# Convolution kernel: normalisation two steps ahead, high parts in front of signs, one more pair of products split by columns

## The reference: two layers on eight images

```python
def _L0_conv_ref(x, depthwise_weights, pointwise_weights, attention_weights, global_attention_weight):
    dw = lax.conv_general_dilated(x, depthwise_weights, ..., feature_group_count=C)   # 3x3, padding 1
    A = jax.nn.softmax(attention_weights, axis=1)
    att = jnp.einsum('cd,bdhw->bchw', A, dw)
    pw = jnp.einsum('kc,bchw->bkhw', pointwise_weights[:, :, 0, 0], att)
    G = jax.nn.softmax(global_attention_weight, axis=1)
    return jnp.einsum('cd,bdhw->bchw', G, pw)

def _L1_conv_ref(x, w):
    xb = jnp.sign(x)
    wc = jnp.clip(w, -1.0, 1.0)
    mean_val = jnp.mean(jnp.abs(wc), axis=(1, 2, 3), keepdims=True)
    bw = jnp.sign(wc) * mean_val
    return lax.conv_general_dilated(xb, bw, ...)                                      # 3x3, padding 1

x = x + _L0_conv_ref(_gn(x), ...)
x = x + _L1_conv_ref(_gn(x), L1_conv_w)
```

## Time and profile before

| | |
|---|---|
| median of three runs | 1948.15 us |
| the profiled execution's own time | 1947.49 us |
| its span | 1945.5 us |
| TensorE matmul | 1807.5 us busy (93%), 35562 matmuls |
| TensorE weight load | 1531.9 us (79%) |
| VectorE | 1667.6 us (86%) |
| ScalarE | 1275.6 us (66%) |
| GpSimd | 535.5 us (28%) |
| DMA | mean 140 GB/s |
| chain that ended last | PE 82%, VectorE 9%, SyncE's queue 3%, issue 3%, ScalarE 2% |

### The profile page before, as it was taken

One profiled execution on the slowest core, in us unless ns is written; L12 is line 12 of the kernel. 1 busy time (PEld: TensorE's weight loads), 2 busy tenths in 40 slices (PEclk: granted clock), 3 DMA queues, 4 the chain that ended last, 5 costly groups with the idle time before them and its releaser, 6 DMA issues.

```text
span 1945.5 us, 81090 instructions
## 1 busy us (share of the span) xinstructions
PE 1807.5 (93%) x35562; PEld 1531.9 (79%) x35562; DVE 1667.6 (86%) x2578; ACT 1275.6 (66%) x1367; POOL 535.5 (28%) x285
## 2 busy tenths in 40 slices
PE   0099999999999999999999999999999999999997
PEld 0077777988876776899978787799997777799996
DVE  5568889888898889888898888988889888988887
ACT  2066776777666776677766677677766677677774
POOL 0032222223222222222222232223323222232221
PEclk9999999999999999999999999999999999999999
DMA  9925555555655565556555556556655565433223
GB/s 205 220 68 152 151 151 133 152 157 152 151 126 153 151 151 142 142 152 151 151 131 153 141 151 151 132 150 155 152 151 136 151 151 151 106 78 76 76 76 99
DMA packets 279270, 271.50 MB, mean 140 GB/s; under 512 B 16576, under 2 KB 278848, under 8 KB 279104
## 3 DMA queue, kind: packets, MB, share of 16 engines
q1 hardware_dynamic: 279104, 269.23, 55.1%
HBM read 134.95 MB, written 134.22 MB: 138 GB/s over the span
## 4 chain that ended last, share of the span: by engine, by line
PE 82%; DVE 9%; SPq 3%; issue 3%; ACT 2%; DMA 1%; DVEq 0%; ACTq 0%
PE psA L484 71%; PE psB L484 11%; SPq L249 3%; DVE ring L850 1%; DVE bnt L685 1%; ACT xh L365 1%; DVE ring L876 1%; DVE aggr L791 1%; DVE xc L842 1%; DVE sums L697 1%; DVE psL L878 1%; DMA ring<-in_x 1%; ACT xn L361 1%; DVE ring L882 1%; SPq L256 0%
## 5 line engine op out<-in xcount | busy, mean ns | idle before, releaser
L484 PE MATMUL psA<-xh,W 64*64 64x512 f16 (+1 forms) x19456 | 1670.5, 361 | 37.3 <-ACT xh L365 30.8
L484 PEld LDWEIGHTS psA<-xh,W 64*64 64x64 f16 x19456 | 1176.2, 106 | 194.7 <-issue 50.7
L484 PE MATMUL psA<-xl,W 64*64 64x512 f16 (+1 forms) x9984 | 1144.8, 361 | 0.3 <-issue 0.3
L301 POOL TENSOR_TENSOR xl<-xc,xn 128x1024 f16<-128x1024 f32 (+2 forms) x264 | 532.6, 2019 | 1331.4 <-ACT xn L361 1331.4
L484 PEld LDWEIGHTS psA<-xl,W 64*64 64x64 f16 x9984 | 635.0, 106 | 81.9 <-issue 1.5
L484 PE MATMUL psB<-pk,W 64*64 64x512 f16 (+3 forms) x5568 | 638.0, 341 | 3.4 <-DVE pk L861 2.3
L384 ACT ACTIVATE sg<-ring,columns 128x1024 f16<-128x1024 f32 (+2 forms) x270 | 297.3, 1106 | 510.8 <-DVE ring L850 494.4
L365 ACT ACTIVATE xh<-xc 64x1024 f16<-64x1024 f32 (+1 forms) x528 | 543.1, 1031 | 9.5
L850 DVE SCALAR_TENSOR_TENSOR ring<-psA,columns,ring 128x1024 f32<-128x1024 f32 x256 | 328.5, 1283 | 213.0 <-PE psA L484 213.0
L484 PEld LDWEIGHTS psB<-pk,W 64*64 64x64 f16 x5568 | 340.9, 106 | 29.1 <-issue 9.1
L685 DVE BATCH_NORM_STATS2 bnt<-ring 128x6 f32<-128x512 f32 x512 | 326.5, 680 | 0.1
(11 more groups left out here) (90 smaller groups left out, 139.1 us busy)
## 6 DMA issues: line engine op xcount, KB each, us to landing
out_y<-ring SPq DMA_DIRECT2D x512, 256.0 KB, 3.2
ring<-in_x SPq DMA_DIRECT2D x448, 256.0 KB, 4.0
ring<-in_x SPq DMA_DIRECT2D x32, 512.0 KB, 13.9
pk<-in_w1T SPq DMA_DIRECT2D x2, 144.0 KB, 8.0
ring<-in_w1n SPq DMA_DIRECT2D x2, 144.0 KB, 7.9
grp<-in_same_group SPq DMA_DIRECT2D x1, 64.0 KB, 6.2
ring<-in_dw SPq DMA_DIRECT2D x2, 2.2 KB, 5.8
ring<-in_att SPq DMA_DIRECT2D x1, 16.0 KB, 2.0
```

The costliest lines, as they stand in the source:

```text
L301: ins = nc.gpsimd.tensor_tensor(xl[:, slot:slot + rows, 1:W + 1], xc[:, j:j + rows], xn[:, k:k + rows, 1:W + 1], ALU.subtract)
L484: mm = pe.matmul(bank[out0:out0 + C, c0:c1], weights[src0:src0 + C, :], src[src0:src0 + C, slot:slot + rows, width[0]:width[0] + width[1]] ...
```

## The change

Three things are done.

1. VectorE normalises chunk t + 2 at the end of step t, and no longer chunk t + 1 behind `add_layer0`. `add_layer1` becomes `add_left` (L878 and L882's work) and `add_right` (L876's work) with `take_part` between them, and the border instructions of `take_part` come behind its statistics. The statistics between images now stand behind `pack`.
2. ScalarE makes the high part of chunk t + 1 ahead of the signs of chunk t - 2.
3. On TensorE a straight pair of group 1 (`beside`, part 0, dx = 1) is cut by columns in every step with a layer-1 part. Its first 256 columns go to the crossing side as `beside_plain_first`, its last 256 stay on the straight side as `beside_second`. The straight side then has 28 whole layer-0 pairs, 3 sign pairs and one half, the crossing side 25, 6 and one half: 31.5 rounds on either.

```diff
             for t in range(ALL):
+                if t + 1 < ALL:
+                    high_of(t + 1)
                 if t + 1 >= LAG:
                     signs_of(t + 1 - LAG)
-                if t + 1 < ALL:
-                    high_of(t + 1)
...
+            def beside_plain_first(ch, dx):
+                k = G * ch.par
+                return pair(True, psA[:, ch.par, 2 * W:3 * W], xn, dx, W, (W0[:, 0, dx, 1, :], [(k, 1, 0, W)]),
+                            (W0[:, 0, dx, 0, :], [(k + 2, 1, 0, W)]), False, False)
+
+            def beside_second(ch, dx):
+                bank = psA[:, ch.par, 3 * W:4 * W]
+                wt = W0[:, 0, dx]
+                mm = piece(0, 0, bank, wt[:, 3, :], xh, columns(ch, 2, 1, W), (dx, W), False, False)
+                if not ch.at(NC - 1):
+                    mm = piece(C, C, bank, wt[:, 2, :], xh, columns(ch, 4, 1, W), (dx, W), False, False)
+                return mm
...
             def step_one(img, a, img1, u, between=None):
                 layer0_begins(img, a)
                 for k in range(32):
-                    if k < 13:
-                        crossing_layer0(img, a, k, 1)
-                    elif k < 19:
-                        crossing_signs(img1, u, k - 13)
-                    elif k < 31:
-                        crossing_layer0(img, a, k - 6, 1)
+                    if k < 14:
+                        crossing_layer0(img, a, k, True)
+                    elif k < 20:
+                        crossing_signs(img1, u, k - 14)
+                    else:
+                        crossing_layer0(img, a, k - 6, True)
...
             normalise(*of(0))
+            normalise(*of(1))
             for t in range(ALL):
                 img, a = divmod(t, NC)
                 if t > 0:
                     add_layer0(*of(t - 1))
-                if t + 1 < ALL:
-                    normalise(*of(t + 1))
                 if t > LAG:
-                    add_layer1(*of(t - LAG - 1))
+                    add_left(*of(t - LAG - 1))
                 for g in parts_at(t):
                     if g < ALL:
                         take_part(g)
+                if t > LAG:
+                    add_right(*of(t - LAG - 1))
+                if a == 0:
+                    mean_of_x1(img)
+                if t + 1 >= LAG:
+                    pack(*of(t + 1 - LAG))
                 if img + 1 < NB:
                     if a == AGGR_STEP:
                         stats_parts(img + 1)
...
-                if a == 0:
-                    mean_of_x1(img)
-                if t + 1 >= LAG:
-                    pack(*of(t + 1 - LAG))
+                if t + 2 < ALL:
+                    normalise(*of(t + 2))
```

More of the change, by code:

```diff
@@ L571, in crossing_layer0 @@
                     mm = beside_plain(a, 0)
+                elif g == 1 and i == 13:
+                    mm = beside_plain_first(a, 1)
                 elif i < 6:
@@ L635, in step_one @@
                     else:
[L636 removed]
+                        straight_layer0(img, a, k - 3, True)
                     if between is not None and k == 10:
```

57 lines of the change are left out of this document (33 added, 24 removed).

## The result

The changed kernel took 1915.89 us, the median of four runs (1914.05 to 1923.54), against 1947.36 for the kernel before (four runs, 1945.4 to 1950.78). The ratio is 0.985, 95% interval 0.983 to 0.987: faster by 1.5%. The forecast was 1896, with a range up to 1924. The direction came out as forecast, and so did both mechanisms, the half round and the boundary; the time is 20 us above the forecast, and most of what follows is about those 20 us.

The account below looks back on a forecast made before the run. The prediction took TensorE's straight side, 32 rounds a step, as the bound. From 1947.5 us it took 26.3 for the half pair and 25.2 for the boundaries, giving 1896.0, with a range of 1883 to 1924.

Parts of the forecast that it names:

- What bounds the kernel: Steady step: TensorE's straight side, 32 rounds in 6.94 us, is the bound; VectorE, ScalarE and GpSimd have slack.
- The half pair: TensorE's straight side: a half slot saves 0.104 us in 253 of 256 steps, 26.3 us in all.
- Rival 1: TensorE's two sides run in step, so a half beside a whole costs a whole: 1922 us, chance 0.13.
- The waits on TensorE: Straight side, places 15 and 21, waiting for crossing pairs two rounds earlier: 0.16 us of margin, cost taken as nothing.
- Rival 3: The two waits at distance two empty TensorE every step, up to 0.3 us each: slower, 2048 us, chance 0.05.
- Order on VectorE and ScalarE: Steady step: `xh` done 3.2 us in, its slack from 0.45 to 2.7; `pack` 0.69; VectorE 0.9 us free.
- The boundary: Between images: one TensorE wait of 2.0 us; seven boundaries lose 17.4 us against 42.6, a gain of 25.2.
- Half a fall at each boundary: Granted clock falling behind TensorE's boundary wait: half of 1.7 us, 0.85, counted at each of six boundaries.
- Rival 2: The wait only moves to the new image's first chunk and the clock falls each time: 1921 us, chance 0.13.
- The hitches: Single stops on TensorE that nobody on the other engines causes: 7.8 us, claimed to stay.

## Why the prediction was right, and which term was mis-sized

**What bounds the kernel.** Right. TensorE's round sets the step: 32 rounds are 6.94 us, 31.5 are 6.83, with either order of the other engines (the runs with the order alone and the half pair alone).

**The half pair.** The term is right, 26.3 predicted and 253 x 0.104 measured, and yet the half pair is worth nothing in the changed kernel: the order alone has ratio 0.983 and the whole change 0.985. The hitches that it brings eat what it saves. Kept out of the written-out steps it pays, 0.977. Rival 1 is refuted by the 0.11 us between the half pair and its successor beside a whole round. The rule of the Trainium skill behind it (page "TensorE: Matmul & The Clock Gate", section "Measured speedup vs the span model") would have kept the step at 6.94; for these quarter-array sides the trace does not agree.

**The waits on TensorE.** Right. No start of a matmul is more than 0.18 us behind the last one between 1150 and 1165 us, so neither place 15 nor place 21 empties TensorE. Rival 3 is refuted.

**Order on VectorE and ScalarE.** Right: `xh` 3.26 us after the step's start (3.2 predicted), `pack` 0.70 (0.69), 0.86 us of slack (0.9). But it rested on a pair of edits that I treated as separate. That GpSimd's part ends early was used only for `pack`, 0.2 us. The run with VectorE's order alone shows what else hung on it, 1.5 us of L910.

**The boundary.** Right in its steps, a little off in its size. The second boundary, which has no hitch, in VectorE's timeline:

```profile
527.27 1.28 DVE L871 SCALAR_TENSOR_TENSOR ring<-psA,columns,ring 128x1024 f32<-128x1024 f32 x1 [0.86 <-PE psA L484]
...
531.55 0.16 DVE L717 COPY sums<-ring 64x2 f32<-64x2 f32 x1
...
536.13 1.28 DVE L871 SCALAR_TENSOR_TENSOR ring<-psA,columns,ring 128x1024 f32<-128x1024 f32 x1
...
543.52 1.28 DVE L871 SCALAR_TENSOR_TENSOR ring<-psA,columns,ring 128x1024 f32<-128x1024 f32 x1
...
551.24 1.28 DVE L871 SCALAR_TENSOR_TENSOR ring<-psA,columns,ring 128x1024 f32<-128x1024 f32 x1
...
577.10 1.28 DVE L871 SCALAR_TENSOR_TENSOR ring<-psA,columns,ring 128x1024 f32<-128x1024 f32 x1
```

ScalarE there:

```profile
537.33 2.13 ACT L365 ACTIVATE xh<-xc 64x1024 f16<-64x1024 f32 x2
...
552.75 2.74 ACT L365 ACTIVATE xh<-xc 64x256 f16<-64x256 f32 x4
```

And TensorE:

```profile
555.64 1.51 PE L484 MATMUL psA<-xh,W 64*64 64x512 f16 x36 [0.64 <-ACT xh L365]
```

From 527.27, steps start at 8.86 and 16.25 (predicted 8.8 and 16.5), chunk 30's `xh` is done at 12.19 (12.0) and the new image's first at 28.22 (28.4). Seven steps take 49.83 us, 2.0 over 7 x 6.833. The border copy takes 0.16, where it took 1.29. The prediction took 0.5 us for the two border instructions as an estimate, and the trace has the reason why it holds. GpSimd, at the boundary of rows 6 and at this one:

```profile
988.71 2.07 POOL L301 TENSOR_TENSOR xl<-xc,xn 128x1024 f16<-128x1024 f32 x1 [5.05 <-ACT xn L361]
```

```profile
528.45 2.07 POOL L301 TENSOR_TENSOR xl<-xc,xn 128x1024 f16<-128x1024 f32 x1 [4.77 <-ACT xn L361]
```

In the kernel before, the copy starts at 989.51 beside this instruction and ends at 990.80, 0.02 us after it (990.78). Now it starts at 531.55, when GpSimd is done (530.52). So 1.1 us of VectorE's time came back in each of two steps of a full boundary, by the place of the copy against GpSimd. What I had wrong is the look of the loss: TensorE starts the new image 2.0 us late, as worked, but stands quite still for only 0.64 of it, since the products of the old image stretch into that time. So the sum of waits for `xh` is 2.5 and not near 12, and I have not split the rest of the 2.0. The stretch behind it, busy us of PE, PEld, DVE, ACT and POOL, then clock, which answers to the earlier trace rows:

```profile
555.60:559.00 3.40, 3.36 (x73) 2.91 (x77) 2.67 (x4) 2.40 (x3) 0.00 (x0) 1.00 0.73 163
```

The clock stays at full speed, as at the other boundaries of this execution (its mean granted clock is 0.999). The kernel's other three executions have 0.997, so falls are not gone for good; where they stand is not on record. In the profiled executions of the other runs with the whole new order that have falls ahead of the program's end (seven falls in five runs), each fall stands within 1.1 us of the end of a hitch of 1.9 to 3.2 us, and none at a wait for `xh`; the changed kernel's own longest hitch, 2.3 us, has none beside it. Half a fall at each boundary was counted, 5.1 us in all. Without it the forecast for the seven would have been 12.3; 13.4 were measured, since the last one loses 1.7 and not 0.3, 0.4 of it by its hitch. Rival 2 is refuted; the run with the order alone says the same, with 1.3 lost at a boundary without a hitch.

**The hitches.** Here the prediction failed: "The single hitches stay." They were 7.8 us and became 32.0, a term of +24.2 that the sum put at nothing. I had them as a constant of the program because no engine causes them, and did not ask what does. With the other two terms as measured and this one at nothing, the sum is 1892. That 1916 still lies inside the stated range (1883 to 1924) is luck: its upper end was set by rivals 1 and 2, which are both refuted, and the measured time is nearer to their 1922 and 1921 than to the forecast. The mechanism, as far as it is shown: they are TensorE's instruction blocks that arrive late (multiples of 256 instructions), late behind data (issue 26.6, 12.6, 3.9 with fewer bytes), only in code that is written out (no hitch in later passes of a loop; 12.6 when the half pair is kept out of the written-out steps). What most likely brings them up is the change's own success: a step uses up its instructions in 6.83 us in place of 6.94 and has two more matmuls and two more weight loads, so each block in written-out code costs a little more of the packets' lead. With 32 rounds and the same instructions issue is 11.5. What is not shown is how a block's packet is ordered against the data packets, and why the half pair brings 17 us of issue with the new order and 10 without it.

## What to carry to other kernels

Idle time that the profile puts down to "issue" is a cost with a cause: count the engine's instructions between two such gaps, and if they are multiples of one block, weigh each instruction added to written-out code, and each microsecond taken off it, against the data transfers beside it. An edit in a hardware loop meets it only in the loop's first pass. And before an order is judged by its parts, ask of each instruction which engine it runs beside: here both parts alone were slower by 2 to 4% and the two together faster by 1.7%, for one of VectorE's instructions had come to lie beside GpSimd's, and the other order moves GpSimd's away.

## What the runs showed of the hardware that was not expected

A VectorE instruction with two inputs in SBUF (L910 reads `rnd` and `ring`) is held while GpSimd's L301 reads SBUF: 2.26 us in place of 0.74 when it starts 0.35 behind GpSimd, 1.22 when it meets its last 0.67. It ends about 0.55 us behind GpSimd's instruction in both (0.54 and 1157.02 - 1156.47). The same explains the 0.88 of `pack` in the kernel before, whose two inputs are both in `sg`: it ended at 1161.13, 0.54 behind the end of this GpSimd instruction in the kernel before (1160.59).

```profile
1158.51 2.08 POOL L301 TENSOR_TENSOR xl<-xc,xn 128x1024 f16<-128x1024 f32 x1 [4.85 <-ACT xn L361]
```

The Trainium skill, page "SBUF — State Buffer", section "Who interferes with whom", says that such an instruction and a GpSimd instruction that reads SBUF exclude each other; the runs agree. A copy with one input (64 x 2 elements, the border copy of the kernel before) is held as well: it meets GpSimd's L301 in 13 of its 16 executions, takes 1.10 to 1.29 us there in place of 0.15, and ends 0.02 us behind it. L905 has one input in PSUM and one in SBUF and takes 0.75 beside GpSimd (1154.93 in the changed kernel, with GpSimd at work from 1154.19 to 1156.26), as it does without.

Two sides of quarter-array matmuls keep their own time to half a round. And TensorE can lose 0.2 to 2.3 us at one block of instructions, 23 times in a program, at full granted clock.
